# Windowed attention on one Trainium2 core: the mask added by VectorE instead of TensorE, and the token transposes moved within the step

## The reference

```python
DEPTH, HEADS, DIM_HEAD, WINDOW = 6, 16, 64, 32
# per layer, q and k from x @ Wqkv, normalised and rotated, v from the same product:
bk2, bv2 = (look(bk), look(bv))               # each window sees its own and the previous 32 keys
mask = (it < jb) | (it > jb + w) | (jb == -1)
sim = jnp.einsum('bhwie,bhwje->bhwij', bq, bk2) * QK_SCALE
sim = jnp.where(mask, -jnp.finfo(sim.dtype).max, sim)
attn = jax.nn.softmax(sim, -1)
out = jnp.einsum('bhwij,bhwje->bhwie', attn, bv2)
x = x + out @ Wo                               # then x + ffn_layer(x), gated GELU, inner 341
```

## Time and profile before

| | |
|---|---|
| median of the runs | 5577.74 us |
| the profiled execution: its own time | 5584.4 us |
| its span | 5582.6 us |
| TensorE matmul, share of the span | 89% |
| VectorE | 62% |
| GpSimd | 50% |
| ScalarE | 43% |
| mean granted TensorE clock | 0.94 |
| windowed stages, about | 871 to 2715 us and 3672 to 5548 us |

### The profile page before, as it was taken

One profiled execution on the slowest core, in us unless ns is written; L12 is line 12 of the kernel. 1 busy time (PEld: TensorE's weight loads), 2 busy tenths in 40 slices (PEclk: granted clock), 3 DMA queues, 4 the chain that ended last, 5 costly groups with the idle time before them and its releaser, 6 DMA issues. The chain is left out here.

```text
span 5582.6 us, 126260 instructions
## 1 busy us (share of the span) xinstructions
PE 4985.9 (89%) x52272; PEld 3451.1 (62%) x52272; DVE 3450.7 (62%) x4560; ACT 2420.3 (43%) x2934; POOL 2813.2 (50%) x3652
## 2 busy tenths in 40 slices
PE   7788887999999999999778888879999999999997
PEld 3344434666666666666467777646666666666664
DVE  1477816666666666666356666356666666666663
ACT  2333323555555555555222111035555555555553
POOL 0100006767776777777112111057677777677772
PEclk9899998999999999999779999689999999999998
DMA  0000001000000000000000000010000000000000
GB/s 12 6 0 0 0 4 46 9 9 14 9 14 10 14 9 6 2 2 2 8 1 0 0 0 0 1 46 9 9 14 9 14 10 12 11 2 6 2 2 9
DMA packets 15198, 46.20 MB, mean 8 GB/s; under 512 B 4192, under 2 KB 7008, under 8 KB 12896
## 3 DMA queue, kind: packets, MB, share of 16 engines
q1 hardware_dynamic: 14688, 38.93, 2.0%
HBM read 37.87 MB, written 1.05 MB: 7 GB/s over the span
## 5 line engine op out<-in xcount | busy, mean ns | idle before, releaser
L725 POOL TENSOR_TENSOR w_qk<-w_turned 128x1024 f32<-128x1024 f32 x384 | 905.1, 2357 | 315.0 <-DVE w_turned L608 259.9
L603 DVE TENSOR_TENSOR w_turned<-w_ps_qk,w_rot_l 128x1024 f32<-128x1024 f32 x384 | 469.9, 1224 | 881.4 <-ACT w_squares L509 862.0
L307 PE MATMUL w_ps_y<-w_px,w_w_vo 128*128 128x128 f32 x6144 | 809.7, 288 | 141.2 <-ACT w_px L513 135.9
L307 PEld LDWEIGHTS w_ps_y<-w_px,w_w_vo 128*128 128x128 f32 x6144 | 764.1, 202 | 192.5 <-ACT w_px L513 166.7
L257 PE MATMUL w_ps_qk<-w_w_qk,ZT 128*128 128x512 f32 x1536 | 740.0, 605 | 36.5 <-DVE w_turned L608 15.4
L754 POOL TENSOR_TENSOR w_qk<-w_qk,w_inv_norm 128x1024 f32<-128x1024 f32 x384 | 722.9, 1904 | 0.0
L509 ACT ACTIVATE w_squares<-w_ps_qk 128x1024 f32<-128x1024 f32 x384 | 391.7, 1020 | 545.9 <-PE w_ps_qk L257 545.8
L608 DVE TENSOR_TENSOR w_turned<-w_ps_qk,w_rot_l 128x1024 f32<-128x1024 f32 x384 | 466.6, 1215 | 0.0
L612 DVE TENSOR_REDUCE w_sumsq<-w_squares 128x16 f32<-128x1024 f32 x384 | 455.5, 1186 | 0.0
L263 PE MATMUL w_ps_t<-ident,w_qk 128*128 128x128 f32 x3072 | 425.4, 283 | 7.7 <-ACT w_qT L538 7.2
L513 ACT ACTIVATE w_px<-w_ps_t 128x1024 f32<-128x1024 f32 x192 | 196.7, 1025 | 508.1 <-PE w_ps_t L299 508.1
(11 more groups left out here) (254 smaller groups left out, 9412.0 us busy)
## 6 DMA issues: line engine op xcount, KB each, us to landing
w_w_qk<-in_w_qk SPq DMA_DIRECT2D x12, 1024.0 KB, 4.8
w_w_vT<-in_w_vT SPq DMA_DIRECT2D x12, 512.0 KB, 3.7
w_w_o<-in_w_o SPq DMA_DIRECT2D x12, 512.0 KB, 4.6
w_w<-in_w SPq DMA_DIRECT2D x12, 384.0 KB, 3.1
w_w<-in_w SPq DMA_DIRECT2D x12, 192.0 KB, 3.1
XT<-in_x SPq DMA_DIRECT2D x1, 1024.0 KB, 4.8
w_rot<-in_rot SPq DMA_DIRECT2D x2, 512.0 KB, 5.8
out<-XT SPq DMA_DIRECT2D x1, 1024.0 KB, 3.9
```

The lines of the kernel that those rows point to most:

```text
L307: last = nc.tensor.matmul(ps_y[:, D.t * P:(D.t + 1) * P].rearrange("p (a v q) -> p a v q", a=2, q=WIN), w_vo[:, D.parity, h, p, :], px[:, ...
L603: nc.vector.tensor_tensor(turned[:, which, 0, :].rearrange("p (h d) -> p h d", d=DH), flat(ps_qk[:]).rearrange("p (h d) -> p h d", d=DH), ...
L725: nc.gpsimd.tensor_tensor(qk[:, T.odd, which, :], turned[:, which, 0, :], turned[:, which, 1, :], ALU.add).then_inc(pool_add, 1)
```

## The change

Two edits. First, `scores` no longer writes the mask: the 128 small matmuls start their accumulation themselves. VectorE adds the fp32 mask (`mask_in`, in SBUF) to `ps_s` and writes the sum to `probs` in SBUF; the maximum is taken from `probs`, and the subtraction reads `probs` and `neg_max` and writes `probs`. Second, the four token transposes of B stand in `place_0` (before the first half of `output`) in the bc, gate and up steps, and stay in `place_4` in the down step. The two edge transposes go to the end of the gate step. The copy of the token windows follows them on ScalarE: between `qT` and `kT` in three of four steps. `x_win` gets a slot for each of the four tiles.

```diff
             def scores(B):
-                for a in range(2):
-                    nc.tensor.matmul(ps_s[:, a, :], ident_b[:],
-                                     spread(mask[:, min(B.t, 1), :], 1, [P, HEADS // 2, KEYS]),
-                                     start=True, stop=False, skip_group_check=True)
...
-                                start=False, stop=True, skip_group_check=True)
+                                start=True, stop=True, skip_group_check=True)
...
+            def tokens(s):
+                if s.C:
+                    pe.wait_ge(act_xt, s.B.n)
+                windows(s.B, s.B.col - WIN, WINS, pe_xt)
+
             def place_0(s):
-                if s.edge:
...
-                    windows(s.edge, s.edge.col - 3 * WIN, 2, pe_xe)
                 if s.down:
...
+                elif s.B and s.k % TILES:
+                    if s.gate:
+                        pe.wait_ge(dve_xn, s.gate.m + 1)
...
+                    if s.k % TILES == 3:
+                        pe.wait_ge(act_xe, s.B.batch + 1)
...
+                    tokens(s)
...
             def place_4(s):
+                if s.B and s.k % TILES == 0:
                     if s.cen:
                         pe.wait_ge(dve_var, s.cen.m + 1)
+                    tokens(s)
+                if s.edge:
+                    if s.gate:
                         pe.wait_ge(act_gate, s.gate.m * FFB + FFB)
...
+                    windows(s.edge, s.edge.col - 3 * WIN, 2, pe_xe)
...
                 if D:
                     if C:
-                        pe.wait_ge(dve_sub, C.n + 1)
+                        pe.wait_ge(dve_mask, C.n + 1)
                     gather(D, 1, ps_s)
...
+            def tokens_out(B, C):
+                act.wait_ge(pe_xt, B.n + 1)
+                nc.scalar.activation(flat(x_win[:, WINS * B.t:WINS * (B.t + 1), :]), ps_f[:], ACT.Copy).then_inc(act_xt, 1)
...
                 if B:
                     dve.wait_ge(pe_s, B.n + 1)
-                    nc.vector.tensor_reduce(neg_max[:], ps_heads, AXX, ALU.max, negate=True).then_inc(dve_max, 1)
+                    if C:
+                        dve.wait_ge(pe_pt, C.n + 1)
+                    by_half = lambda ap: ap.rearrange("p (h c) k -> p h c k", h=2)
+                    nc.vector.tensor_tensor(probs[:].rearrange("p (c h) k -> p h c k", h=2), by_half(ps_heads),
+                                            by_half(spread(mask[:, min(B.t, 1), :], 1, [P, HEADS, KEYS])),
+                                            ALU.add).then_inc(dve_mask, 1)
...
                 if B:
-                    if C:
-                        dve.wait_ge(pe_pt, C.n + 1)
+                    dve.wait_ge(dve_mask, B.n + 1)
+                    nc.vector.tensor_reduce(neg_max[:], probs[:], AXX, ALU.max, negate=True).then_inc(dve_max, 1)
                     dve.wait_ge(dve_max, B.n + 1)
-                    by_half = lambda ap: ap.rearrange("p (h c) k -> p h c k", h=2)
-                    nc.vector.tensor_tensor(probs[:].rearrange("p (c h) k -> p h c k", h=2), by_half(ps_heads),
-                                            by_half(spread(neg_max[:], 2, [P, HEADS, KEYS])),
+                    nc.vector.tensor_tensor(probs[:], probs[:], spread(neg_max[:], 2, [P, HEADS, KEYS]),
                                             ALU.add).then_inc(dve_sub, 1)
```

More of the change, by code:

```diff
@@ L75, in __init__ @@
         self.y, self.cen, self.bc, self.gate, self.up, self.down = [self.rows(at) for at in range(7, 13)]
-        self.edge = self.A if self.A and self.A.t == 0 else None
+        self.edge = self.B if self.B and self.B.t == 0 else None
     def tile(self, age):
@@ L142, in windowed_layers @@
     tag = f"w{run}"
-    ident, ident_b, mask = consts["ident"], consts["ident_b"], consts["mask"]
+    ident, mask = consts["ident"], consts["mask_in"]
     centre, mean_col = consts["centre"], consts["mean_col"]
@@ L214, in slot @@
         def slot(C, w, h):
-            if h == 0 or w >= 2:
-                return WINS * C.odd + w - 2 * h
-            return 2 * WINS + w if C.t == 0 else WINS * (1 - C.odd) + w + 2
+            return TILES * WINS + w if h and w < 2 and C.t == 0 else WINS * C.t + w - 2 * h
         block = ctx.enter_context(nc.Block())
@@ L358, in place_1 @@
                 if s.cen:
-                    if s.C:
-                        pe.wait_ge(act_xt, s.C.n + 1)
                     if s.down:
                         pe.wait_ge(dve_z, s.down.m + 1)
+                    elif s.C:
+                        pe.wait_ge(act_xt, s.C.n + 1)
                     pe.wait_ge(dve_y, s.cen.m + 1)
@@ L413, in place_4 @@
             def place_4(s):
[L414 to L417, removed]
+                if s.B and s.k % TILES == 0:
                     if s.cen:
                         pe.wait_ge(dve_var, s.cen.m + 1)
-                    elif s.bc:
-                        pe.wait_ge(dve_xn, s.bc.m + 1)
-                    elif s.gate:
+                    tokens(s)
+                if s.edge:
+                    if s.gate:
                         pe.wait_ge(act_gate, s.gate.m * FFB + FFB)
-                    elif s.up:
-                        pe.wait_ge(dve_hid, s.up.m * FFB + FFB)
                     elif s.k == 2:
                         pe.wait_ge(dve_bias, L0 + 1)
[L428 to L431, removed]
+                    else:
+                        pe.wait_ge(act_xt, s.B.n + 1)
+                    windows(s.edge, s.edge.col - 3 * WIN, 2, pe_xe)
             def gate(f, i):
@@ L486, in step @@
                 if B:
[L487 to L491, removed]
+                    if not C:
+                        pe.wait_ge(act_tk, B.n + 1)
+                    elif not D:
+                        pe.wait_ge(dve_mask, C.n + 1)
                     scores(B)
@@ L538, in step @@
                     nc.scalar.activation(flat(qT[:]), flat(ps_t[:]), ACT.Copy).then_inc(act_tq, 1)
[L539 to L543, removed]
+                    if s.k % TILES:
+                        tokens_out(B, C)
                     act.wait_ge(pe_tk, B.n + 1)
@@ L573, in step @@
                     gathered(C, 0, ps_t)
+                if B and s.k % TILES == 0:
+                    tokens_out(B, C)
+                if s.edge:
+                    act.wait_ge(pe_xe, s.edge.batch + 1)
+                    nc.scalar.activation(flat(x_win[:, TILES * WINS:TILES * WINS + 2, :]), ps_f[:, 0:2 * P],
+                                         ACT.Copy).then_inc(act_xe, 1)
                 if B:
-                    act.wait_ge(pe_xt, B.n + 1)
-                    nc.scalar.activation(flat(x_win[:, WINS * B.odd:WINS * (B.odd + 1), :]), ps_f[:],
-                                         ACT.Copy).then_inc(act_xt, 1)
                     act.wait_ge(dve_sub, B.n + 1)
@@ L1843, in _ @@
                 dve.wait_ge(ready, 8)
-        consts = dict(ident=ident, ident_b=ident_b, mean_w=mean_w, mask=mask, eps=eps, one=one, centre=centre,
+        consts = dict(ident=ident, ident_b=ident_b, mask_in=mask_in, mean_w=mean_w, mask=mask, eps=eps, one=one, centre=centre,
                       mean_col=mean_col)
```

28 lines of the change are left out of this document (8 added, 20 removed).

## The result

The changed kernel takes 5602.05 us (median of 6 runs, 5595.97 to 5614.54), the kernel before 5585.55 beside it (6 runs). The ratio is 1.0034, with a 95% interval of 1.0021 to 1.0047: slower by 12 to 26 us. Forecast was 1.0047 (5604 on 5577.7), the upper end of that interval. The profiled execution has a span of 5594.1 us (before 5582.6) and a mean clock of 0.942.

What follows compares the result with a forecast made beforehand. TensorE is nearly always busy, but ScalarE's px, hanging on VectorE's subtraction, decides. Per call, rounds of four steps add 9.6 us, head and tail 4; two calls +27 on 5577.7: about 5604 us, range 5545 to 5635.

Steps and rivals of the forecast that it cites:

- The reading that TensorE is busy and yet does not set the pace: Windowed stretches: TensorE 94% busy, yet ScalarE's px comes just in time, hanging on VectorE's subtraction by under 1 us.
- Walk, down step: Down step into bc step: subtraction 0.90 us late, taken by the slack; mask's 0.53 us saving lost; +0.03 us.
- Plain bc step: Plain bc step into gate step: later probs and subtraction delay the exponential and output; +1.39 us.
- the slack of 0.54: Bc step: 0.54 us between the subtraction's end and the exponential's start, subtracted from the subtraction's lateness.
- Bias: Bc step with bias product: same as plain, but 0.7 us of it was there before.
- Gate: Gate step into up step: turn_probs +0.3, scores -0.23, subtraction +1.0 against a slack of 0.96; +0.1 us.
- Up: Up step: transposes gone from its end, -0.49 us; output 0.12 us late behind the down matmuls; -0.37 us.
- Merge: Bc step with a merge: probs is no wait and L725 ends before the subtraction; +0.05 us in place of 1.39.
- The lock: Plain and bias bc steps: VectorE's two-SBUF-input subtraction waits for GpSimd's L725; 0.3 us a seam, 8 of 27 us.
- the rival of the wide lock: Down and gate steps: subtraction also waits for GpSimd, 0.5 us in each of 96 steps, +48 us, 5652; chance 0.12.
- TensorE's clock: Half-rate stretches after idle time, some 50 of up to 1.6 us, about 80 us at stake; no change taken, 25 us either side.
- The move of the transposes: Token transposes, 0.49 us, hidden where TensorE waits for px: at most 24 us over 48 gate-to-up seams.

Runs made afterwards that it cites:

- e5: Kernel before without the two mask matmuls and nothing in their place, so it computes another result: 5506.49 us, 0.9871.
- e6: Kernel before with one more 1024-wide VectorE addition behind the maximum in each step, written to a spare tile; mask stays on TensorE: 5723.21 us, 1.0250.
- e3: Changed kernel with the masked sum written back to PSUM and gather(D, 1) waiting for the subtraction again: 5615.18 us, 1.0064.
- e1: Kernel before with the mask edit alone (mask added on VectorE); token transposes and their copy left in place: 5638.51 us, 1.0100.
- e2: Changed kernel with the mask back on TensorE, so only the token transposes and their copy are moved: 5515.51 us, 0.9880.
- e9: Kernel before with ScalarE's exponential moved behind the next step's qT copy and GELU behind kT; transposes not moved: 5400.07 us, 0.9684.
- e10: Changed kernel with the mask back on TensorE, ScalarE's exponential moved behind the next step's qT copy and GELU behind kT: 5352.17 us, 0.9596.
- e7: Changed kernel with ScalarE's exponential alone moved behind the next step's qT copy; GELU stays ahead of the square and px: 5488.9 us, 0.9848.

## Why the prediction was right

**The reading that TensorE is busy and yet does not set the pace** held in part: the mask's move costs about 60 us alone, although up to 102 us of TensorE's work was on offer. But e5 shows that 72 of these 102 us do count when VectorE pays nothing. TensorE and the chain of VectorE and ScalarE end close together in most steps, so time taken from one counts only until the other is reached, and time added to the other counts as well. The mask's move loses because its price on VectorE (some 130 us, the estimate under e6) is higher than these 72 us.

**Walk, down step** (+0.03): seam -0.05 in the median. **Plain bc step** (+1.39): +1.37 by the median seam, +1.40 by the mean, 1.39 by the rows; its parts, `probs` 0.9 late, the lock, the slack of 0.54 used up, all show. **Bias** (+0.7): +0.68. **Gate** (+0.1): +0.11. **Up** (-0.37): -0.49 between the shortest frequent seams, those with no half-rate stretch (19.05 before, 18.56 after); the term was mis-sized by the table load.

**Merge** (+0.05): +0.41. This step of the walk failed in size. The merge step that I measured in the trace was one of 18.6 us, with a short pause among the score matmuls; the usual one has 18.23. Over 16 rounds that is 5 us.

**The lock** was placed in plain and bias rounds, 0.3 us each, 8 us. There it is 0.20. I missed ten gate steps in which GpSimd folds the next layer's scales behind L716, and the subtraction runs into them:

```profile
1893.42 0.74 POOL L703 TENSOR_TENSOR w_rot_l<-w_rot,w_qk_scale 128x256 f32<-128x256 f32 x1
1893.46 1.78 DVE L675 TENSOR_TENSOR w_probs<-w_probs,w_neg_max 128x1024 f32<-128x1024 f32 x1
```

It takes up to 1.78 us there, and up to 1.95 in the head: 14 us of VectorE's time in all. So the rival of the wide lock came true in these steps alone; in the down steps of the full pipeline the subtraction took its usual 1.22 us. These rows agree with the Trainium skill's rule (SBUF — State Buffer, section "SBUF: two separate sides"): the subtraction ends 1.08 to 1.09 us after the GpSimd operation at hand, nearly its whole 1.22 us, and does not run at a shared rate beside it. e3 agrees as well: the rule names two SBUF inputs as the condition, and e3's subtraction, with one, never waits.

**How near the median came is in part luck.** The forecast of 5604 us and the measured 5602 us stand on different medians of the kernel before: +27 us on 5577.7 was forecast, +16.5 us on 5585.55 came (12 to 26 by the interval). With the table's differences, and -0.49 us a seam for the up steps, the walk gives a loss of 31 us; 15 stand in the seams of the profiled execution. The missing 16 us lie in the long up seams (before, 29 of 42 lay above 19.9 us; after, 25). I put their length down to half-rate stretches like the one shown above; not every one was looked at. The forecast put 25 us to either side for TensorE's clock; that it gave some back is not a step that I foresaw, and one profile each can't show whether the change itself does it.

**The move of the transposes** was valued at the up step alone (24 us at most). It is worth 67 us without the mask's move, and about 36 with it (e1 against the changed kernel). In the forecast for the whole change this was no visible error. A likely reason, not tested apart: the walk took the bc and gate seams from the chain of VectorE and ScalarE, behind which the same transposes are hidden. In the expectation for e2 it was a large error.

## What to carry to other kernels

An engine at 94% can still be paced from outside in some of its steps: look for the slack between each producer's end and its consumer's start on the path back to the busy engine, and set an added operation against the slack, not against the busy share. Walk each kind of step on its own, since what TensorE gains in one is lost to another engine's limit in the next. And look at what stands in an in-order queue ahead of the copy that the busy engine waits for: moving ScalarE's exponential and GELU behind it gave 3% on the kernel before (e9), more than either part of the change, and 4% together with the transposes' move (e10). Split a change with a small result into its parts, as one may be worth keeping.

## What the runs showed that I had not expected

A gap of 0.26 us on TensorE behind eight transposes shows in no matmul row as idle, since the modelled matmul ends reach over it. Start-to-start times against the same pair elsewhere reveal it (1.19 against 0.93 us), and so does the wait in the row of the weight load.

The table load of ScalarE starts before the operation that the activation behind it waits for has ended (2068.40 against 2069.42).

With the idle time ahead of `output` in the up step cut from 2.81 to 1.39 us by e7, `output` took 2.05 us there, at a granted clock of 1.00:

```profile
2014.52 2.05 PE L301 MATMUL w_ps_y<-w_px,w_w_vo 128*128 128x128 f32 x16 [1.39 <-ACT w_px L497]
```

In e7 one of 42 up seams lies above 19.9 us, in the changed kernel 25. 36 of e7's last 17.77 to 17.79 us, against 18.56 in the changed kernel, but this part is no gain: in e7 `qT`, the mark, comes earlier in the down step (0.20 us behind the start of `down` on TensorE, not 1.32), and the down seam is about as much longer (18.33 against 17.49 us). Up and down seams together are 46 us shorter in e7, and the bc seams 33. The gate seams gave 20 us, where 50 were expected (1.2 us in 42). So e7 came near its expectation in sum, and not in its parts.
